# Sums by destination with two PSUM pairs for the slot results and the placement one step ahead

## The chip, the cores and the metric

The kernel runs on one core of one Trainium2 chip. The metric is the device time of one execution in microseconds (us). Three runs of the kernel before took 5358.63, 5363.5 and 5366.24 us, median 5363.5.

## The reference

Four graph layers run over one graph of 100,000 nodes with 16 features and 50,000 edges; each ends in `x = layernorm(x + layer(x))`. Edges are sorted by destination, and destinations are denser at small node numbers (`dst = 100000 * u**2`).

```python
# layer 0: attention over the edges of a destination (16x16 weights per edge)
e1, e2 = w_m * feat[src], w_a * feat[src]
ft = segment_sum(e1 * softmax_by_dst(e2), dst).sum(axis=1)
# layer 1: bilinear messages, added at the SOURCE node
messages = einsum('eu,ev,uvw->ew', x[row], x[col], W_tp);  out.at[row].add(messages)
# layer 2: two rounds of a graph convolution
agg = segment_sum(x[src], dst);  h = relu((x + agg) @ wa + ba) @ wb + bb      # twice
# layer 3: a 16x16 matrix per edge type (8 types), then a GRU cell
msg = einsum('emh,eh->em', edge_emb[edge_type], features[src])
m = segment_sum(msg, dst);  h_new = gru(m, features)
```

So `segment_sum(table[src], dst)` is computed three times: from the outputs of layer 1, of the first round of layer 2 and of the whole of layer 2. These are the three "sums by destination"; the third one also multiplies every gathered row by the matrix of its edge type.

## The kernel before

Five engines run their own instruction lists, written out by hand and tied by semaphores. Stages follow one another: the attention layer, node passes over 14 tiles of 7168 nodes, a sum by source, then three times a sum by destination followed by a node pass (`sum_by_destination(k)` and `node_steps`, k = 0, 1, 2).

Inside one sum by destination:

* **Gathers (GpSimd, L667).** The 50,176 padded edges stand in 392 tiles of 128. One indirect DMA for each tile fetches the 128 source rows into `dy`. They are issued in 49 groups of eight. Each group has its semaphore; SyncE waits for the group's landing (L583) and raises `tiles_ready`.
* **Slots.** The result lies in `acc` (SBUF) in 98 blocks of 1024 nodes. A slot is a pair of an edge tile and a block into which that tile writes; slots stand in order of tile and block, eight to a slot group, and there are 62 slot groups. Since a tile that crosses a block has two slots, the last slot groups need fewer new tiles than the first.
* **`pick` (ScalarE, L832)** waits until the last tile that its slot group needs is there, loads eight offsets into registers, and copies the eight picked row sets into `ysl[b]`, a PSUM buffer (two of them, in the pair `ps[3]`).
* **`place` (VectorE, L1526)** multiplies the picked rows with a mask, so that each row stands in the columns of its node within a group of eight (`placed[b]`, 128x1024).
* **`one_hot` (VectorE, L1519)** makes the matrix `oneh[b]` that maps an edge to its row of `acc`, from `io_p` in PSUM.
* **`slots` (TensorE, L1085)** multiplies `oneh[b]` by `placed[b]`, eight matmuls in two halves of four, into the PSUM pair `ps[2]`. `slot_ps` is raised after each half. Before each half it waits on `acc_done` until `collect` has read the same half of the slot group before.
* **`collect` (VectorE, L1543)** adds the eight results to `acc` at offsets held in registers, one after the other, each add waiting for the one before.

VectorE's step for slot group c is, in this order: `place(c)`, `one_hot(c+1)`, `collect(c)`. In the first two sums steps 2 to 59 are a hardware loop of two steps a turn, in the third all 62 are written out.

The third sum has for each tile group g also: `place_types(g)` on VectorE (a mask, L1504, then the rows spread over the eight types, L1509, called `zt`; it waits for `tiles_ready`), `turn` on TensorE (L1062, eight transposes into the pair `ps[0]`), `turned` on ScalarE (L807, `ps[0]` to SBUF), `messages` on TensorE (L1072) into `ps[1]` and on ScalarE (L813) back over `dy`. Only then can `pick` copy. Step n holds `place_types(n+3)` on VectorE between `place` and `one_hot`; on TensorE `turn(n+2)`, `messages(n+1)`, `slots(n)` in this order; on ScalarE `turned(n+2)`, `messages(n+1)`, `pick(n+1)`. Tile groups end with `place_types(48)` in step 45, `turn(48)` in step 46 and `messages(48)` in step 47, so steps 48 to 61 have slot work alone.

Of the kernel before, what the change touches and what calls it, by code (L numbers as in the profile page):

```python
# [30 lines left out]
ALU = mybir.AluOpType  # L31
# [3 lines left out]
P = 128  # L35
# [32 lines left out]
SG = 8  # L68
# [28 lines left out]
def build_program(nc, x, ef, wlog, repcon, src_t, dst_t, next_t, src_row, dst_row, prev_row, type_row, first_row,  # L97
# [3 lines left out]
    with ctx:  # L101
# [9 lines left out]
        def dram(name, shape, dt=FP32):  # L111
# [179 lines left out]
            sem(n) for n in ("tmask_done", "zt_done", "ztT_ps", "ztT_sb", "ym_ps", "msg_done"))  # L291
        ACC_ZEROS = 1

        node_in, late_in, stored = pair("node_in"), pair("late_in"), pair("stored")
# [653 lines left out]
        def _(pe):  # L948
# [102 lines left out]
            def sum_by_destination(k):  # L1051
# [24 lines left out]
                def slots(i, c):  # L1076
                    b = c % 2
                    pe.wait_ge(oneh_done, 2 * i + base + c + 1)
                    pe.wait_ge(placed_done, 2 * i + base + c + 1)
                    for h in range(2):  # L1080
                        if later(i, c, 1) or k:
                            pe.wait_ge(acc_done, 2 * SG * i + SG * (base + c - 1) + SG // 2 * (h + 1)
                                       + ACC_ZEROS * (k + later(i, c, 1)))
                        for j in range(SG // 2 * h, SG // 2 * (h + 1)):
                            last = pe.matmul(ps[2][:, j * P:(j + 1) * P], oneh[b][:, j * P:(j + 1) * P],  # L1085
                                             placed[b][:, j * P:(j + 1) * P], start=True, stop=True)
                        last.then_inc(slot_ps, 1)
# [91 lines left out]
        def _(dve):  # L1179
# [303 lines left out]
            def sum_by_destination(k):  # L1483
# [38 lines left out]

                def place(i, c):
                    b = c % 2
                    dve.wait_ge(y_copied, 2 * i + base + c + 1)
# [7 lines left out]
                def collect(i, c):  # L1533
# [4 lines left out]
                    for j in range(SG):  # L1538
# [3 lines left out]
                        o = acc[:, bass.ds(at[j], P)]  # L1542
                        dve.tensor_tensor(o, o, ps[2][:, j * P:(j + 1) * P], ALU.add).then_inc(acc_done, 1)  # L1543

                def step(i, c):
                    place(i, c)
                    if typed:
                        place_types(c + 3)
                    one_hot(i, c + 1)
                    collect(i, c)  # L1550

                if typed:
                    for g in range(3):
                        place_types(g)
                one_hot(0, 0)
                if typed:
                    for n in range(SLOT_GROUPS):
                        step(0, n)
                else:
                    steps(dve, step, 0, 2, SLOT_GROUPS - 2, SLOT_GROUPS)  # L1560
# [213 lines left out]
```

## Time and profile before

| | before |
|---|---|
| median of three runs | 5363.5 us |
| profiled execution | 5358.86 us |
| its span, first to last instruction | 5357.0 us |
| VectorE busy | 3796.2 us (71%) |
| TensorE matmul busy | 3260.3 us (61%) |
| GpSimd busy | 3045.7 us (57%) |
| ScalarE busy | 1645.2 us (31%) |
| mean granted TensorE clock | 0.77 of full |

About 2 us of the profiled execution lie outside its span. Busy shares are averages over stages with different limits. The three sums by destination, which the change touches, take some 530, 530 and 632 us, and in each of them another engine may be the one that the others wait for; the views of those stretches tell which.

### The profile page before, as it was taken

Reading aid. Unit: us, or ns where it says so; the run is one execution under the profiler, and the core shown is the slowest. Engines: PE = TensorE matmul, PEld = TensorE weight load, DVE = VectorE, ACT = ScalarE, POOL = GpSimd, SP = SyncE. Lnnn points to the kernel's source line nnn. Section 1 sums busy time; section 2 is a strip of 40 time slices with the busy share of each in tenths; the row PEclk is TensorE's granted clock in tenths of the full one; section 3 lists DMA queues with packets and bytes.
Section 4 is the critical chain, followed back from the end, with each engine's and each line's share of the span. In section 5 each row is a group of like instructions: output and inputs, shape, how many; then the busy total and the mean of one; then the engine's idle time right before and its main releaser. Section 6 shows DMA issues by size and latency. Waiting matters only on the chain.

```text
span 5357.0 us, 56936 instructions
## 1 busy us (share of the span) xinstructions
PE 3260.3 (61%) x12357; PEld 2396.4 (45%) x12357; DVE 3796.2 (71%) x6342; ACT 1645.2 (31%) x4066; POOL 3045.7 (57%) x2659
## 2 busy tenths in 40 slices
PE   5888888888805344436878444453444544766686
PEld 2444444444405334435767334443344324666432
DVE  5999999999966555536999755644556674555588
ACT  2555555555532111102333101111111341222143
POOL 2666666666612888885555677715777007776000
PEclk9999999999995665558999655676556565666598
DMA  3111111111142444431211000041000320000122
GB/s 93 36 44 42 38 44 41 41 41 44 27 111 53 57 58 62 59 40 36 55 41 51 14 7 7 7 116 35 7 7 7 103 86 10 7 7 7 35 82 75
DMA packets 400935, 231.46 MB, mean 43 GB/s; under 512 B 127626, under 2 KB 365646, under 8 KB 400802
## 3 DMA queue, kind: packets, MB, share of 16 engines
q1 hardware_dynamic: 281522, 210.43, 13.8%
q0 software_dynamic: 119296, 19.68, 6.8%
q8 instruction: 48, 0.79, 0.1%
q14 instruction: 69, 0.57, 0.0%
HBM read 152.10 MB, written 58.54 MB: 39 GB/s over the span
## 4 chain that ended last, share of the span: by engine, by line
POOL 34%; DVE 26%; issue 19%; PE 9%; DMA 6%; ACT 2%; SPq 2%; DVEq 1%; POOLq 0%; ACTq 0%
POOL extra L667 21%; POOL sums L652 9%; DVE arena L1599 4%; POOL xg L630 3%; DMA sums<-cmb,sidx 3%; DVE arena L1323 2%; DVE arena L1347 2%; PE ps L1127 2%; PE ps L994 2%; DMA edge_in<-far_row 2%; POOL ft_t L619 1%; PE ps L1085 1%; DVE arena L1543 1%; DVE ps L1317 1%; DVE arena L1331 1%
## 5 line engine op out<-in xcount | busy, mean ns | idle before, releaser
L1085 PE MATMUL ps<-arena 128*128 128x128 f32 x2976 | 687.0, 424 | 764.2 <-DVE arena L1526 692.7
L667 POOL DMA_INDIRECT extra<-x_t,srci x784 | 780.1, 995 | 527.0 <-issue 527.0
L1085 PEld LDWEIGHTS ps<-arena 128*128 128x128 f32 x2976 | 638.3, 326 | 804.9 <-issue 804.9
L652 POOL DMA_INDIRECT sums<-cmb,sidx x392 | 613.6, 1565 | 336.4 <-ACT cmb L781 204.3
L994 PE MATMUL ps<-edge_in,wl 17*128 17x512 f32 x784 | 704.4, 1076 | 87.3 <-DMA edge_in<-far_row 85.1
L1543 DVE TENSOR_TENSOR arena<-arena,ps 128x128 f32 x1488 | 427.8, 287 | 368.3 <-PE ps L1085 193.1
L630 POOL DMA_INDIRECT xg<-in_x,xidx x392 | 437.5, 1116 | 353.1 <-DVE xp L1305 233.4
L619 POOL DMA_INDIRECT ft_t<-fts,fidx x392 | 506.7, 1293 | 139.2 <-issue 117.6
L1032 PE MATMUL ps<-arena 128*128 128x128 f32 x992 | 226.8, 421 | 521.1 <-DVE arena L1410 521.1
L667 POOL DMA_INDIRECT extra<-h_t,srci x392 | 383.4, 978 | 251.5 <-issue 251.5
L832 ACT ACTIVATE ps<-extra 128x16 f32 x1488 | 171.3, 168 | 1066.1 <-SPq L583 868.6
L994 PEld LDWEIGHTS ps<-edge_in,wl 17*128 17x128 f32 x784 | 243.5, 325 | 479.3 <-issue 352.5
L1032 PEld LDWEIGHTS ps<-arena 128*128 128x128 f32 x992 | 210.7, 323 | 529.4 <-DVE arena L1410 529.4
L1127 PE MATMUL ps<-wb,arena 128*128 128x256 f32 x1568 | 389.9, 406 | 91.8 <-ACT arena L860 76.4
L976 PE MATMUL ps<-cst,arena 128*128 128x16 f32 x1568 | 351.2, 375 | 111.4 <-ACT fts L709 101.0
L976 PEld LDWEIGHTS ps<-cst,arena 128*128 128x128 f32 x1568 | 341.9, 331 | 132.3 <-issue 121.5
L1127 PEld LDWEIGHTS ps<-wb,arena 128*128 128x128 f32 x1568 | 312.2, 204 | 144.4 <-ACT arena L860 95.7
L1526 DVE TENSOR_TENSOR arena<-edge_in,ps 128x1024 f32<-128x1024 f32 (+1 forms) x186 | 226.7, 1219 | 169.1 <-ACT ps L832 159.5
L394 POOL TENSOR_TENSOR extra<-arena 128x512 f32<-128x512 f32 x196 | 203.3, 1058 | 245.1 <-DVE arena L1599 230.2
L1599 DVE TENSOR_REDUCE arena<-extra 128x32 f32<-128x512 f32 x294 | 282.3, 1016 | 0.0
L1323 DVE TENSOR_TENSOR_SCAN arena<-ps,arena,edge_in 128x512 f32<-128x512 f32 x196 | 240.8, 1271 | 13.4
L1519 DVE TENSOR_TENSOR arena<-ps,relp 128x1024 f32<-128x1024 f32 x186 | 226.3, 1216 | 0.1
(200 smaller groups left out, 5978.9 us busy)
## 6 DMA issues: line engine op xcount, KB each, us to landing
edge_in<-far_row SPq DMA_DIRECT2D x98, 256.0 KB
ain<-in_src_row SPq DMA_DIRECT2D x56, 448.0 KB, 3.9
sums<-zero SPq DMA_DIRECT2D x132, 144.0 KB
ain<-arena SPq DMA_DIRECT2D x42, 448.0 KB, 5.2
arena<-rel_t SPq DMA_DIRECT2D x63, 256.0 KB, 4.0
x_t<-yout SPq DMA_DIRECT2D x28, 448.0 KB, 3.3
extra<-x_t,srci POOLq DMA_INDIRECT x784, 2.4
xin<-x_t SPq DMA_DIRECT2D x28, 448.0 KB, 4.7
```

The costliest lines, as they stand in the source:

```text
L619: pool.indirect_dma_start(ft_t, bass.IndirectOffsetOnAxis(ap=fidx[b][:, k:k + 1], axis=0), fts[b][:, k * F:(k + 1) * F], None).then_inc(ft ...
L630: pool.indirect_dma_start(xg[:, k, :], None, x, bass.IndirectOffsetOnAxis(ap=xidx[:, k:k + 1], axis=0)).then_inc(x_gathered, 16)
L652: pool.indirect_dma_start(sums[k], bass.IndirectOffsetOnAxis(ap=sidx[n % 2][:, j:j + 1], axis=0), cmb[n % 2][:, j, :], None, compute_op=AL ...
L667: pool.indirect_dma_start(dy[:, t, :], None, table, bass.IndirectOffsetOnAxis(ap=srci[:, t:t + 1], axis=0)).then_inc(d_gathered[n % QUEUE] ...
L976: last = pe.matmul(ps[3][:, 512 + k * F:512 + (k + 1) * F], rat[b][:, h, k * P:(k + 1) * P], selo, start=h == 0, stop=h == CH - 1)
L994: last = pe.matmul(ps[k][:, h * ET:(h + 1) * ET], wl[:, (k * CH + h) * P:(k * CH + h + 1) * P], eft[b][:, :], start=True, stop=True)
L1032: last = pe.matmul(ps[b][:, j * P:(j + 1) * P], turned_oneh[b][:, j * P:(j + 1) * P], xblk[b][:, j * P:(j + 1) * P], start=True, stop=True)
L1085: last = pe.matmul(ps[2][:, j * P:(j + 1) * P], oneh[b][:, j * P:(j + 1) * P], placed[b][:, j * P:(j + 1) * P], start=True, stop=True)
L1127: last = pe.matmul(bank_of(k)[:, 256 * s:256 * (s + 1)], sT[par_], wbk[j // 4][:, (j % 4) * 256:(j % 4 + 1) * 256], start=True, stop=True)
L1323: last = dve.tensor_tensor_scan(mx[b][:, h, 1:ET + 1], ps[0][:, h * ET:(h + 1) * ET], far[b][:, :], mx[b][:, h, 0:1], ALU.max, ALU.add)
L1543: dve.tensor_tensor(o, o, ps[2][:, j * P:(j + 1) * P], ALU.add).then_inc(acc_done, 1)
L1599: dve.tensor_reduce(slots(zz)[:, s0:s0 + 2, :], ([prod[n_par(c, g)]] + pool_prod)[k].rearrange("p (s u w) -> p s w u", s=2, u=F), AX, ALU. ...
```

## The change

`slot_sums(k, n)` names the PSUM pair into which slot group n of sum k goes. In the first two sums it is `ps[2]` for even and `ps[0]` for odd groups. In the third it is `ps[2]` up to group 50, since `turn` uses `ps[0]`, and from group 51 on the two alternate; the first group in `ps[0]` waits until `ztT_sb` shows that `turned` has read all. `back` is how many groups back the `collect` lies that must have read the pair: 2 where the pairs alternate, else 1.

VectorE's step for slot group c becomes `place(c+1)`, `one_hot(c+2)`, `collect(c)`. `place(0)` and `one_hot(1)` move ahead of the first step. `one_hot(c+2)` writes the buffer that `slots(c)` reads, and waits for both its halves. The picked rows stay in `ysl` in PSUM, as before. No operation is added or removed, only waits change.

```diff
--- before.py
+++ after.py
@@ -290,6 +290,13 @@
         tmask_done, zt_done, ztT_ps, ztT_sb, ym_ps, msg_done = (
             sem(n) for n in ("tmask_done", "zt_done", "ztT_ps", "ztT_sb", "ym_ps", "msg_done"))
         ACC_ZEROS = 1
+        TYPES_DONE = TILE_GROUPS + TILE_GROUPS % 2
+
+        def slot_sums(k, n):
+
+            if k < DST_PASSES - 1:
+                return ps[0] if n % 2 else ps[2]
+            return ps[0] if n > TYPES_DONE and n % 2 else ps[2]
 
         node_in, late_in, stored = pair("node_in"), pair("late_in"), pair("stored")
         v_done, s_own, s_xm, s_sq, s_ve, s_sd, y_done = (
@@ -1075,14 +1082,18 @@
 
                 def slots(i, c):
                     b = c % 2
+                    n = c
+                    back = 2 if not typed or n > TYPES_DONE + 1 else 1
+                    if typed and n == TYPES_DONE + 1:
+                        pe.wait_ge(ztT_sb, TILE_GROUPS)
                     pe.wait_ge(oneh_done, 2 * i + base + c + 1)
                     pe.wait_ge(placed_done, 2 * i + base + c + 1)
                     for h in range(2):
-                        if later(i, c, 1) or k:
-                            pe.wait_ge(acc_done, 2 * SG * i + SG * (base + c - 1) + SG // 2 * (h + 1)
-                                       + ACC_ZEROS * (k + later(i, c, 1)))
+                        if later(i, c, back) or k:
+                            pe.wait_ge(acc_done, 2 * SG * i + SG * (base + c - back) + SG // 2 * (h + 1)
+                                       + ACC_ZEROS * (k + later(i, c, back)))
                         for j in range(SG // 2 * h, SG // 2 * (h + 1)):
-                            last = pe.matmul(ps[2][:, j * P:(j + 1) * P], oneh[b][:, j * P:(j + 1) * P],
+                            last = pe.matmul(slot_sums(k, n)[:, j * P:(j + 1) * P], oneh[b][:, j * P:(j + 1) * P],
                                              placed[b][:, j * P:(j + 1) * P], start=True, stop=True)
                         last.then_inc(slot_ps, 1)
 
@@ -1521,6 +1532,8 @@
                                       ALU.is_equal).then_inc(oneh_done, 1)
 
                 def place(i, c):
+                    if not inside(i, c, SLOT_GROUPS):
+                        return
                     b = c % 2
                     dve.wait_ge(y_copied, 2 * i + base + c + 1)
                     dve.tensor_tensor(
@@ -1540,19 +1553,21 @@
                             dve.wait_ge(slot_ps, 4 * i + 2 * (base + c) + j // (SG // 2) + 1)
                         dve.wait_ge(acc_done, 2 * SG * i + SG * (base + c) + j + ACC_ZEROS * (k + 1))
                         o = acc[:, bass.ds(at[j], P)]
-                        dve.tensor_tensor(o, o, ps[2][:, j * P:(j + 1) * P], ALU.add).then_inc(acc_done, 1)
+                        dve.tensor_tensor(o, o, slot_sums(k, c)[:, j * P:(j + 1) * P], ALU.add).then_inc(acc_done, 1)
 
                 def step(i, c):
-                    place(i, c)
+                    place(i, c + 1)
                     if typed:
                         place_types(c + 3)
-                    one_hot(i, c + 1)
+                    one_hot(i, c + 2)
                     collect(i, c)
 
                 if typed:
                     for g in range(3):
                         place_types(g)
                 one_hot(0, 0)
+                place(0, 0)
+                one_hot(0, 1)
                 if typed:
                     for n in range(SLOT_GROUPS):
                         step(0, n)
```

VectorE at the start of the first sum, before (L1490 clears `acc`, L1492 makes the mask, L1519 is `one_hot`, L1526 `place`, TENSOR_LOAD the offsets for `collect`, ISA a wait, L1543 an add of `collect`):

```order
L1490 MEMSET arena 128x12672
L1492 TENSOR_TENSOR edge_in<-cst,relj 128x3968
L1519 TENSOR_TENSOR arena<-ps1,relp 128x1024
L1526 TENSOR_TENSOR arena<-edge_in,ps3 128x1024
L1519 TENSOR_TENSOR arena<-ps1,relp 128x1024
L1534 TENSOR_LOAD offs
L1543 ISA
L1543 TENSOR_TENSOR arena<-arena,ps2 128x128
```

The same place in the changed kernel (its lines are L1501, L1503, L1530 `one_hot`, L1539 `place`, L1556 `collect`):

```order
L1501 MEMSET arena 128x12672
L1503 TENSOR_TENSOR edge_in<-cst,relj 128x3968
L1530 TENSOR_TENSOR arena<-ps1,relp 128x1024
L1539 TENSOR_TENSOR arena<-edge_in,ps3 128x1024
L1530 TENSOR_TENSOR arena<-ps1,relp 128x1024
L1539 TENSOR_TENSOR arena<-edge_in,ps3 128x1024
L1530 TENSOR_TENSOR arena<-ps1,relp 128x1024
L1547 TENSOR_LOAD offs
L1556 ISA
L1556 TENSOR_TENSOR arena<-arena,ps2 128x128
```

One more `place` and one more `one_hot` stand ahead of the first `collect`, and from there on each `collect` comes behind the placement of the next slot group.

TensorE at the end of the third sum, in the changed kernel (L1079 is `messages(48)`, L1096 `slots`):

```order
L1079 MATMUL ps1<-prm,arena 128x16 x8
L1096 MATMUL ps2<-arena 128x128 x32
L1096 MATMUL ps0<-arena 128x128 x8
L1096 MATMUL ps2<-arena 128x128 x8
L1096 MATMUL ps0<-arena 128x128 x8
L1096 MATMUL ps2<-arena 128x128 x8
L1096 MATMUL ps0<-arena 128x128 x8
L1096 MATMUL ps2<-arena 128x128 x8
```

In the kernel before the last of these rows is a single one:

```order
L1062 MATMUL ps0<-cst,arena 128x128 x8
L1072 MATMUL ps1<-prm,extra 128x16 x8
L1085 MATMUL ps2<-arena 128x128 x8
L1072 MATMUL ps1<-prm,arena 128x16 x8
L1085 MATMUL ps2<-arena 128x128 x120
```

Of the 15 slot groups from 47 on, the four up to 50 still go to `ps2` and the last eleven alternate between the pairs, beginning and ending with `ps0`.

## Rows read from the trace of the kernel before

**Rows 1.** The page, chain that ended last, shares of the span by line.
```profile
POOL extra L667 21%; POOL sums L652 9%; DVE arena L1599 4%; POOL xg L630 3%; DMA sums<-cmb,sidx 3%; DVE arena L1323 2%; DVE arena L1347 2%; PE ps L1127 2%; PE ps L994 2%; DMA edge_in<-far_row 2%; POOL ft_t L619 1%; PE ps L1085 1%; DVE arena L1543 1%; DVE ps L1317 1%; DVE arena L1331 1%
```

**Rows 2.** Windows over the three sums: span; busy PE, PEld, DVE, ACT, POOL; clock.
```profile
3013.00:3543.00 530.00, 228.46 (x992) 211.72 (x992) 301.93 (x622) 56.90 (x496) 383.41 (x392) 0.59 0.08 6
3648.00:4178.00 530.00, 228.14 (x992) 211.36 (x992) 302.06 (x622) 56.91 (x496) 383.38 (x392) 0.58 0.08 6
4425.00:5057.00 632.00, 401.39 (x2168) 381.17 (x2168) 360.66 (x720) 121.17 (x594) 396.64 (x392) 0.61 0.08 6
```

**Rows 3.** Line L667, first and third sum: ns min/median/max, first and last start.
```profile
L667 POOL DMA_INDIRECT extra<-x_t,srci x784: 940/944/14406, 3013.7 to 4939.9; - x196
```

**Rows 4.** Timeline, end of the first sum: start us, us, engine, line, operation.
```profile
3515.34 0.94 POOL L667 DMA_INDIRECT extra<-x_t,srci  x1 [0.30 <-issue]
...
3518.60 0.92 ACT L832 ACTIVATE ps<-extra 128x16 f32 x8 [9.70 <-SPq L583]
...
3521.47 1.22 DVE L1526 TENSOR_TENSOR arena<-edge_in,ps 128x1024 f32<-128x1024 f32 x1
...
3540.66 1.55 DVE L1543 TENSOR_TENSOR arena<-arena,ps 128x128 f32 x4 [0.20 <-PE ps L1085]
```

**Rows 5.** Timeline, end of the second sum.
```profile
4153.55 0.92 ACT L832 ACTIVATE ps<-extra 128x16 f32 x8 [9.76 <-SPq L583]
...
4175.99 1.55 DVE L1543 TENSOR_TENSOR arena<-arena,ps 128x128 f32 x4 [0.20 <-PE ps L1085]
```

**Rows 6.** Timeline, an ordinary step of the third sum.
```profile
4612.85 1.26 DVE L1509 TENSOR_TENSOR arena<-tmask,extra 128x1024 f32<-128x1024 f32 x1 [3.06 <-SPq L583]
...
4614.04 1.21 DVE L1519 TENSOR_TENSOR arena<-ps,relp 128x1024 f32<-128x1024 f32 x1
...
4614.17 1.09 PE L1062 MATMUL ps<-cst,arena 128*128 128x128 f32 x8 [0.66 <-DVE arena L1509]
...
4615.18 1.53 DVE L1543 TENSOR_TENSOR arena<-arena,ps 128x128 f32 x4
...
4619.13 0.92 ACT L832 ACTIVATE ps<-extra 128x16 f32 x8 [1.86 <-issue]
...
4622.76 1.23 DVE L1509 TENSOR_TENSOR arena<-tmask,extra 128x1024 f32<-128x1024 f32 x1 [3.04 <-SPq L583]
4622.85 1.96 POOL L667 DMA_INDIRECT extra<-x_t,srci  x1 [0.30 <-issue]
```

**Rows 7.** Timeline, a step of the third sum in which TensorE ran slower.
```profile
4633.78 1.22 DVE L1509 TENSOR_TENSOR arena<-tmask,extra 128x1024 f32<-128x1024 f32 x1 [4.20 <-SPq L583]
...
4642.47 0.92 ACT L832 ACTIVATE ps<-extra 128x16 f32 x8 [1.89 <-issue]
```

**Rows 8.** Windows over TensorE's turn and messages in those two steps.
```profile
4614.17:4616.96 2.79, 2.79 (x24) 2.69 (x24) 2.20 (x6) 1.02 (x1) 2.18 (x3) 1.00 0.09 6
...
4635.06:4640.26 5.20, 5.20 (x24) 5.09 (x24) 4.21 (x10) 1.03 (x1) 3.98 (x5) 0.50 0.07 5
```

**Rows 9.** Line L1509, tile groups 3 to 48: ns min/median/max, first and last start.
```profile
L1509 DVE TENSOR_TENSOR arena<-tmask,extra x46: 1224/1246/1296, 4480.6 to 4943.1; 128x1024 f32<-128x1024 f32 x46
```

**Rows 10.** Timeline, end of the third sum, with one whole step.
```profile
4951.55 0.92 ACT L832 ACTIVATE ps<-extra 128x16 f32 x8 [1.88 <-issue]
...
4989.29 1.21 DVE L1526 TENSOR_TENSOR arena<-edge_in,ps 128x1024 f32<-128x1024 bf16 x1
4990.42 1.22 DVE L1519 TENSOR_TENSOR arena<-ps,relp 128x1024 f32<-128x1024 f32 x1
...
4990.60 3.76 PE L1085 MATMUL ps<-arena 128*128 128x128 f32 x16 [2.94 <-DVE arena L1526]
...
4992.78 1.54 DVE L1543 TENSOR_TENSOR arena<-arena,ps 128x128 f32 x4 [1.15 <-PE ps L1085]
...
4995.99 1.21 DVE L1526 TENSOR_TENSOR arena<-edge_in,ps 128x1024 f32<-128x1024 bf16 x1
...
5056.80 0.38 SPq L503 DMA_DIRECT2D edge_in<-x_t  x1
```

## The prediction

> **What bounds the kernel now.** I read the chain that ended last first. Its largest entry is the gather of the sums by destination, L667, with 21% of the span [rows 1], three sums of 530, 530 and 632 us [rows 2]. VectorE is busy for 302 of the 530 us, TensorE for 228 [rows 2], so neither fills the first two sums. GpSimd does: one gather takes 0.94 us [rows 3] and 0.30 us pass before the next [rows 4], so 391 gathers at 1.25 us and the first, which takes 14.4 us [rows 3], make 502 us. From 3013.7 [rows 3] that leads to the last one at 3515.3 [rows 4]. What VectorE does faster before that moment is worth nothing. What counts is how long each sum goes on after its last gather: to 3542.2 in the first (3540.66 + 1.55), to 4177.5 in the second [rows 5]. The third starts its last `zt` (tile group 48) at 4943.1 [rows 9] and ends at 5056.8 [rows 10]: 113.7 us, long after the last gather. That tail is where slot work alone sets the time.
>
> **The slot step and what the change saves on it.** In the tail a step lasts from one `place` to the next, 4989.29 to 4995.99, 6.70 us [rows 10]. In it `one_hot` starts 1.13 us after `place` and ends at 4991.64. TensorE starts at 4990.60, once `place` is done, and `collect` begins only at 4992.78, 1.15 us idle for the first four products; from there to the next `place` 3.21 us pass [rows 10]. Where the products are ready, `collect` starts 1.14 us after `one_hot` (4614.04 to 4615.18) [rows 6]. So a step that never waits takes 1.13 + 1.14 + 3.21 = 5.48 us, 1.22 less. With the pairs alternating and `place` one step ahead, TensorE has a whole step of 5.48 us for its 3.76 us [rows 10]; it isn't the limit.
>
> *Third sum, tail.* I count from the start of `collect(50)` to the end.
> - Before: three starts of `collect` lie between steps 50 and 53, and the full step of [rows 10] is step 52 (place(52) at 4989.29, ten places before the end). Going back two steps from 4992.78 gives 4979.4, so 77.4 us to the end.
> - Until group 50 there is one pair. `slots(n)` can then start its halves behind those of `collect(n-1)`: 1.55 + 0.15 us after that start, 3.76 us long, and only then `one_hot(n+2)`, whose buffer it read, 1.14 us before `collect(n)`: 1.70 + 3.76 + 0.1 + 1.14 = 6.7 us. So steps 47 to 51 gain nothing, the wait only moves from `collect` to `one_hot`.
> - From group 52 the step is 5.48. Steps 52 to 59 are eight: 43.8 us. Step 60 has no `one_hot`: 3.21 + 1.2 = 4.4. For the last, the offsets are loaded with nothing beside it (I take 0.5 us): 3.7, and its own adds 3.3. With the 6.7 of step 51 this is 61.9 us, 15.5 less.
> - Against it, `place(47)` now stands a step earlier than the rows it needs. `pick(47)` ends at 4951.55 + 0.92 = 4952.47 [rows 10]; `collect(46)` then starts at 4952.6 + 2.27 = 4954.9. Before, counting back six steps of 6.7 from 4992.78, it starts at 4952.6 at most, its `place` 3.5 us ahead, so VectorE now waits some 4 us for the pick. Some 2.5 us late, which nothing behind it makes up.
> - Net: 13 us less.
>
> *First and second sum, tail.* The last group of tiles frees `pick(59)`, which ends at 3518.60 + 0.92 = 3519.5, and `place(59)` starts at 3521.5 since VectorE is still in the step before [rows 4]: 22.7 us from that pick to the end. After the change VectorE waits there instead: place(59) at 3519.65, `collect(58)` 2.27 later, `collect(59)` 5.5 on, `collect(60)` 4.6 (a loop's end of 0.2 in it), `collect(61)` 3.7 and 3.3 for its adds: 19.5 us, 3.2 less, although there is one more `collect` behind the last pick. Likewise the second: 4153.55 + 0.92 to 4177.5 is 23.1 [rows 5], so 3.6 less. Together 6.8. The bounds: at least 0, if the added collect eats it all, and 9 if steps overlap better than I count.
>
> *Third sum, up to `zt(48)`.* The moved `place(n+1)` stands ahead of the `zt` that waits for the gathers, so `pick` must now be early enough. In the ordinary step the pick that follows a `zt` at 4612.85 ends at 4620.05, 7.2 us on [rows 6]; `place` (0.12 + 1.13) and the mask (0.3) bring the next `zt` to 8.8 us at the earliest. The gathers allow one `zt` in (4943.1 - 4480.6)/45 = 10.28 us [rows 9]. With TensorE slower, the pick ends at 4643.39, 9.6 us after the `zt` [rows 7], and the next `zt` would be 11.2 us on. The difference is TensorE's clock: the same 24 instructions took 2.79 us at 2.4 GHz (1.00) and 5.20 us at 1.2 GHz (0.50) [rows 8]. If a share p of steps is slow, 8.8 + 2.4 p exceeds 10.28 beyond p = 0.6. Before, slow steps are the minority, and the mean clock of this sum is 0.61 [rows 2]. Now `slots(n)` follows `messages(n+1)` at once instead of 2.7 us later, and TensorE then idles in one piece of 2 to 4 us up to the next `turn`. I take that slow and ordinary steps mix about evenly: nothing gained, 1 us lost. Bounds: 45 x (11.2 - 10.28) = 41 us lost, and 13 us gained if all stalls of the gathers (below) vanish.
>
> The Trainium skill (TensorE: Matmul & The Clock Gate, section "HAM oscillation — how this bites in real kernels") says that pauses between batches of matmuls throttle the engine again and again. By this rule, which speaks against gathering the idle time, the `turn` would always start slow. The sum up to `zt(48)` would then be the 41 us bound.
>
> **Sum.** -13 - 6.8 + 1 = -18.8 us. The profiled execution took 5358.9, 2 us more than its span and 4.6 us under the median of the runs. Against the median of 5363.5 the forecast is 5345 us.
>
> **The rivals.**
> *A, the late pick becomes the bound of the third sum.* Every step before `zt(48)` runs at the lower clock and lasts 11.2 us: +41 - 19.8 = +21, 5385 us. For it: the freed time lies in one idle piece ahead of `turn`, and in [rows 7, 8] such a step exists. Against it: `turn`, `messages` and `slots` now form one unbroken block of 7 to 9 us, the most continuous work TensorE has had in this sum. It decides from p = 0.6 on. 12 in 100.
>
> *B, more gathers stall.* A gather issued 0.09 us after a `zt` started took 1.96 instead of 0.94 us [rows 6], and in the third sum the gathers were busy 396.6 against 383.4 us in the others [rows 2]: 13.2 us of such stalls. `place`, `one_hot` and `collect` each have an operand in PSUM, and the first two sums, which have only these, have no stall. At present `zt` starts where a gather has just been issued, mostly a hair late for the next. If late picks move it by some tenths of a us, each of the 45 may meet a gather in its middle and hold it for 0.6 us, half of its own 1.25: 27 us instead of 13, so 14 us later. Then 5345 + 14 = 5359, within 0.2% of before. 17 in 100.
> The Trainium skill (SBUF — State Buffer, section "SBUF: two separate sides") says that a VectorE operation with two SBUF inputs and a GpSimd operation that reads SBUF exclude each other for the whole instruction. The trace agrees for the `zt`; its 14.4 us for the first gather beside the clearing of `acc` fits too [rows 3].
>
> *C, fewer stalls.* The same shift moves `zt` past the gather that it now hits. Then up to 13 us more come off, 5334 us. 13 in 100.
>
> *D, it doesn't do what it says,* since the first two sums gain nothing and the third's last steps go on waiting, for `one_hot` or for TensorE at 3.76 us a group: 5345 + 13 = 5358. 8 in 100: eight steps of 5.48 would have to be near 6.7.
>
> **How the numbers follow.** Forecast 50, A 12, B 17, C 13, D 8. The range reaches from C to just above B: 5334 to 5366 us. About what a measurement of this kernel can tell from no change is 0.2%, 10.7 us. Faster than 5352.8: forecast and C, and a bit of B and D, less the upper part of the forecast: 0.67. Slower than 5374: A, 0.11. The rest, 0.22, is the same.
>
> **What will show it.** In the third sum's tail, places from step 53 on about 5.5 us apart and adds of `collect` with no idle time ahead of them; steps 47 to 51 still 6.7 apart. `place(47)` behind its pick with some 4 us idle. The last `zt` within a few us of 4943 relative to the start of that sum at 4425. The end of the first sum about 19.5 us after the pick of its last tiles. I'm wrong if the `zt`s of the third sum lie more than 10.5 us apart on average, with `place` waiting for `pick` ahead of each (A), if L667 is busy for over 405 us there (B) or under 390 (C).

## The result, and the profile after

The changed kernel took 5348.37 us (median of 20 runs, 5338.56 to 5356.92), the kernel before 5361.15 us beside it (20 runs, 5354.73 to 5372.6). The ratio is 0.9974, 95% interval 0.9968 to 0.9981: 14 us (10 to 17) faster. Forecast were 5345 us and 18.8 us less. The profiled execution took 5352.29 us, its span is 5350.5 us.

Lines have moved: gathers are L674, SyncE's wait L590, `turned` L814, `pick` L839, `turn` L1069, `messages` L1079, `slots` L1096, `zt` L1520, `one_hot` L1530, `place` L1539, `collect` L1556.

The chain that ended last is of less use here. Its shares add up to a fifth of the span only, so its 8% for the gathers can't be held against the 21% in [rows 1]; their busy time did not fall.

```profile
POOL 8%; DVE 7%; issue 4%; PE 2%; ACT 1%; DMA 0%; DVEq 0%; ACTq 0%; POOLq 0%; SPq 0%
```

So I read windows over the three sums, as in [rows 2] (stretch; its length; busy PE, PEld, DVE, ACT, POOL; granted clock; DMA share; GB/s), and the starts of gathers and of `zt` (ns min/median/max, first and last start), as in [rows 3, 9]:

```profile
3010.00:3540.00 530.00, 217.46 (x992) 201.41 (x992) 296.04 (x622) 56.90 (x496) 383.35 (x392) 0.60 0.08 8
3640.00:4170.00 530.00, 220.41 (x992) 204.04 (x992) 295.90 (x622) 56.88 (x496) 383.34 (x392) 0.60 0.08 8
4413.00:5053.00 640.00, 442.99 (x2168) 425.56 (x2168) 363.89 (x720) 121.16 (x594) 412.84 (x392) 0.60 0.07 7
```

```profile
L674 POOL DMA_INDIRECT extra<-x_t,srci x784: 940/944/14414, 3010.2 to 4945.1; - x196
L1520 DVE TENSOR_TENSOR arena<-tmask,extra x49: 1224/1225/1291, 4438.8 to 4948.3; 128x1024 f32<-128x1024 f32 x49
...
  SPq L590: 48.1, 23
```

The last line is the time that VectorE sat idle ahead of these `zt`s for SyncE's word that the gathers had landed, and how often. The kernel before had:

```profile
  SPq L583: 188.3, 49
```

GpSimd is as busy as before in the first two sums, and 16.2 us busier in the third (412.84 against 396.64). From the third sum's first gather (4414.0, 4425.0 before) to its last `zt` it is now 534.3 us, 518.1 before: the same 16.2 us. Of the 49 `zt`s 23 still wait for gathers; before, all 49 did.

The end of the first sum, for [rows 4], and of the second, for [rows 5]:

```profile
3515.07 0.92 ACT L839 ACTIVATE ps<-extra 128x16 f32 x8 [9.65 <-SPq L590]
3516.16 1.22 DVE L1539 TENSOR_TENSOR arena<-edge_in,ps 128x1024 f32<-128x1024 f32 x1 [4.11 <-ACT ps L839]
...
3518.43 3.21 DVE L1556 TENSOR_TENSOR arena<-arena,ps 128x128 f32 x8
...
3523.85 3.21 DVE L1556 TENSOR_TENSOR arena<-arena,ps 128x128 f32 x8
...
3533.77 1.54 DVE L1556 TENSOR_TENSOR arena<-arena,ps 128x128 f32 x4 [0.20 <-DVE arena L1556]
...
4144.94 0.92 ACT L839 ACTIVATE ps<-extra 128x16 f32 x8 [9.79 <-SPq L590]
...
4163.57 1.54 DVE L1556 TENSOR_TENSOR arena<-arena,ps 128x128 f32 x4 [0.20 <-DVE arena L1556]
```

VectorE, 4.1 us idle, now waits for the pick instead of arriving late; from the pick's end (3515.99) to the last add (3535.31) it is 19.3 us, and in the second sum 19.25. They were 22.7 and 23.1.

The tail of the third sum, for [rows 10]: `place(47)` behind its pick, a step before group 51, then an ordinary step and the end.

```profile
4957.00 0.92 ACT L839 ACTIVATE ps<-extra 128x16 f32 x8 [1.87 <-issue]
4957.95 1.22 DVE L1539 TENSOR_TENSOR arena<-edge_in,ps 128x1024 f32<-128x1024 bf16 x1 [4.05 <-ACT ps L839]
...
4963.42 1.21 DVE L1539 TENSOR_TENSOR arena<-edge_in,ps 128x1024 f32<-128x1024 bf16 x1
...
4965.34 1.23 DVE L1530 TENSOR_TENSOR arena<-ps,relp 128x1024 f32<-128x1024 f32 x1 [0.71 <-PE ps L1096]
...
4969.68 1.21 DVE L1539 TENSOR_TENSOR arena<-edge_in,ps 128x1024 f32<-128x1024 bf16 x1
...
5023.85 1.21 DVE L1539 TENSOR_TENSOR arena<-edge_in,ps 128x1024 f32<-128x1024 bf16 x1
5024.98 1.22 DVE L1530 TENSOR_TENSOR arena<-ps,relp 128x1024 f32<-128x1024 f32 x1
...
5026.11 1.53 DVE L1556 TENSOR_TENSOR arena<-arena,ps 128x128 f32 x4
...
5029.31 1.21 DVE L1539 TENSOR_TENSOR arena<-edge_in,ps 128x1024 f32<-128x1024 bf16 x1
...
5048.85 0.38 SPq L510 DMA_DIRECT2D edge_in<-x_t  x1
```

The step is 5.46 us (5023.85 to 5029.31), and `collect` follows `one_hot` without idle time. Ahead of group 51 it is 6.26 here and up to 6.9 later: the idle time stands ahead of `one_hot`. From the last `zt` to the end it is 100.5 us, 113.7 before.

So the tails gave back 3.4 + 3.8 + 13.2 = 20.4 us, and in this pair of executions the stretch before the last `zt` took 16.2 of them. The measured gain is 14 us. The spans differ by 6.5 us, 5357.0 against 5350.5; the 2.3 us beyond that 4.2 lie outside the sums. What the 16.2 us are is the question of the experiments.

### The profile page after: what moved, and what is told of

Read it like the earlier page. It is cut to its first block and busy times, and to the rows that moved or that the text cites. A ratio compares the mean times of both kernels' runs of the same rounds, so it can differ in the third digit from the quotient of the medians.

```text
span 5350.5 us, 56879 instructions
## 1 busy us (share of the span) xinstructions
PE 3291.9 (62%) x12357; PEld 2431.8 (45%) x12357; DVE 3786.6 (71%) x6342; ACT 1645.3 (31%) x4066; POOL 3062.1 (57%) x2659
## 5 line engine op out<-in xcount | busy, mean ns | idle before, releaser
L674 POOL DMA_INDIRECT extra<-x_t,srci x784 | 796.2, 1016 | 524.7 <-issue 524.7
L1096 PE MATMUL ps<-arena 128*128 128x128 f32 x2976 | 661.0, 412 | 667.0 <-DVE arena L1539 603.4
L1096 PEld LDWEIGHTS ps<-arena 128*128 128x128 f32 x2976 | 614.6, 314 | 703.1 <-issue 699.8
L1539 DVE TENSOR_TENSOR arena<-edge_in,ps 128x1024 f32<-128x1024 f32 (+1 forms) x186 | 226.9, 1220 | 496.5 <-ACT ps L839 489.9
L1556 DVE TENSOR_TENSOR arena<-arena,ps 128x128 f32 x1488 | 425.8, 286 | 179.6 <-DVE arena L1556 18.8
L1039 PE MATMUL ps<-arena 128*128 128x128 f32 x992 | 228.1, 423 | 511.7 <-DVE arena L1421 511.7
L674 POOL DMA_INDIRECT extra<-h_t,srci x392 | 383.3, 978 | 246.5 <-issue 246.5
L839 ACT ACTIVATE ps<-extra 128x16 f32 x1488 | 171.2, 168 | 1055.7 <-SPq L590 874.5
L1039 PEld LDWEIGHTS ps<-arena 128*128 128x128 f32 x992 | 211.4, 324 | 520.2 <-DVE arena L1421 520.2
L1530 DVE TENSOR_TENSOR arena<-ps,relp 128x1024 f32<-128x1024 f32 x186 | 226.3, 1217 | 4.8 <-PE ps L1096 4.7
```

Source lines behind the costliest of these rows:

```text
L674: pool.indirect_dma_start(dy[:, t, :], None, table, bass.IndirectOffsetOnAxis(ap=srci[:, t:t + 1], axis=0)).then_inc(d_gathered[n % QUEUE] ...
L1039: last = pe.matmul(ps[b][:, j * P:(j + 1) * P], turned_oneh[b][:, j * P:(j + 1) * P], xblk[b][:, j * P:(j + 1) * P], start=True, stop=True)
L1096: last = pe.matmul(slot_sums(k, n)[:, j * P:(j + 1) * P], oneh[b][:, j * P:(j + 1) * P], placed[b][:, j * P:(j + 1) * P], start=True, stop ...
L1556: dve.tensor_tensor(o, o, slot_sums(k, c)[:, j * P:(j + 1) * P], ALU.add).then_inc(acc_done, 1)
```

## The experiments

A gather is called stalled when it takes longer than the usual 0.944 us. The expectations name four theories:

* **Theory S:** in the third sum a `zt` holds back a gather issued while it runs, since `zt` reads two operands in SBUF. In the expectations of e1 to e4 it also says that the new order brings more of this.
* **Theory B:** that second half alone, under its own name from f_after on.
* **Theory V:** how often it happens is a draw of each execution, not the work of the new order.
* **Theory C:** with placement ahead the pick's own chain (`zt`, `turn`, `messages`, `pick`, `place`) limits the typed steps of the third sum, those that hold a `place_types`.

The table is worked out from the traces, in us. "Gathers": busy time of the 392 gathers of the third sum. "Last zt": from the first gather of that sum to the start of the last `zt`. "Ends": from the pick of the last tiles to the last add, first and second sum. "Tail": from the last `zt` to the last add.

| kernel | gathers | last zt | ends | tail | ratio to before, interval |
|---|---|---|---|---|---|
| before | 396.6 | 518.1 | 22.7, 23.1 | 113.7 | 1 |
| changed | 412.8 | 534.3 | 19.3, 19.3 | 100.5 | 0.9974 (0.9968, 0.9981) |
| f_after (the same again) | 408.8 | 530.9 | 19.4, 19.3 | 100.9 | 0.9969 (0.9958, 0.9981) |
| e1_late_switch | 404.9 | 526.4 | 19.3, 19.3 | 100.9 | 0.9968 (0.9956, 0.9980) |
| e2_first_two_only | 410.5 | 531.9 | 19.3, 19.3 | 113.2 | 0.9993 (0.9984, 1.0002) |
| e3_ahead_one_pair | 412.1 | 533.6 | 20.6, 20.5 | 110.1 | 0.9993 (0.9983, 1.0002) |
| e4_pairs_old_order | 414.8 | 536.3 | 22.7, 23.2 | 112.5 | 0.9995 (0.9986, 1.0004) |
| f6_before_mask_psum | 383.3 | 504.8 | 22.7, 22.9 | 113.6 | 0.9954 (0.9941, 0.9968) |
| f5_after_mask_psum | 383.6 | 508.8 | 19.3, 19.3 | 101.0 | 0.9929 (0.9915, 0.9943) |
| f8_late_psum_49 | 383.3 | 504.8 | 19.4, 19.3 | 97.8 | 0.9916 (0.9902, 0.9929) |

### e1_late_switch and e2_first_two_only: the old order in the third sum

e1 keeps the old order there up to step 46 and places ahead from 47; e2 keeps it to the end, and one PSUM pair with it. In both the `place(0)` and `one_hot(1)` ahead of the first step are left out in the third sum (not in the cuts shown).

```diff
 # e1_late_switch
-                        step(0, n)
+                        if n < 47:
+                            place(0, n)
+                            place_types(n + 3)
+                            one_hot(0, n + 1)
+                            collect(0, n)
+                        else:
+                            if n == 47:
+                                place(0, n)
+                                one_hot(0, n + 1)
+                            step(0, n)
 # e2_first_two_only
-        TYPES_DONE = TILE_GROUPS + TILE_GROUPS % 2
+        TYPES_DONE = SLOT_GROUPS
...
-                        step(0, n)
+                        place(0, n)
+                        place_types(n + 3)
+                        one_hot(0, n + 1)
+                        collect(0, n)
```

> The third sum keeps the old order (place(n), zt, one_hot(n+1)) up to step 46 and places ahead only from step 47 on; all else as changed. Theory S (stalled gathers: zt, started by the pick instead of by the landing, holds up more gathers): L667's gathers in the third sum are busy 397 +-4 us instead of 412.8, the last zt lies 518 +-4 us after the first gather instead of 534, the tail from it stays at 101 +-2, so some 13 to 19 us come off the changed kernel: ratio to before 0.9960 +-0.0010. Theory C (the late pick itself bounds the step): the same place of the last zt, since the pick is off the path again; this run doesn't part S and C. Theory V (chance: the two profiles fell on different draws): gathers 405 to 413 us here too, ratio 0.9974.

> Two pairs and placement ahead in the first two sums alone, the third sum as before. All theories that take the tail of the first two sums for the gain: 19.3 us instead of 22.7 and 23.1 from the pick of the last tiles to the end, 7 us together, ratio 0.9987 +-0.0007. The third sum 632 +-5 us, its gathers 397 +-4 us busy. If the first two sums' gain were eaten somewhere (rival), ratio 1.0000.

Measured: e1 has the changed kernel's tail (100.9) and its ratio; expected under S were gathers of 397 us and 0.9960. e2 keeps the old tail (113.2) and 3.8 us of gain (interval -1 to 9), where the two ends are worth 7. But their gathers were busy for 404.9 and 410.5 us with the order of the kernel before, which had shown 396.6. So it isn't the new order that brings such stalls: the old order has them too, and theory S as it then stood, with about 397 for both kernels, failed.

### e3_ahead_one_pair and e4_pairs_old_order: each half of the change alone

```diff
 # e3_ahead_one_pair
-        TYPES_DONE = TILE_GROUPS + TILE_GROUPS % 2
+        TYPES_DONE = SLOT_GROUPS
...
-                return ps[0] if n % 2 else ps[2]
-            return ps[0] if n > TYPES_DONE and n % 2 else ps[2]
+                return ps[2]
+            return ps[2]
...
-                    back = 2 if not typed or n > TYPES_DONE + 1 else 1
+                    back = 1
 # e4_pairs_old_order
-                    place(i, c + 1)
+                    place(i, c)
...
-                    one_hot(i, c + 2)
+                    one_hot(i, c + 1)
...
-                place(0, 0)
-                one_hot(0, 1)
```

> Placement one step ahead in all three sums, but every slot result in the one pair ps2. My theory (both parts are needed): the wait moves from collect to one_hot, steps of the third sum's tail stay 6.6 to 6.7 us apart, the end of that sum lies 113 us or more behind its last zt, and the gathers are busy 405 to 415 us as in the changed kernel. The first two sums gain 0 to -1 us each at their ends. Ratio 1.0020 to 1.0040, slower than before. Rival (placement ahead alone brings the gain, the pairs nothing): tail steps of 5.5 us, ratio 0.9975.

> Two pairs as in the changed kernel, but VectorE in the old order (place(c), one_hot(c+1), collect(c)). My theory: slots(c) still can't start before place(c), 1.3 us after it, so each tail step stays 6.7 us, the gathers are busy 397 +-4 us, ratio 1.0000 +-0.0007. Rival (the pairs alone bring the gain): tail steps of 5.5 us, ratio 0.9965.

A step in the tail of e3 (placement ahead, one pair), and one of e4 (two pairs, the old order):

```profile
5020.58 1.21 DVE L1539 TENSOR_TENSOR arena<-edge_in,ps 128x1024 f32<-128x1024 bf16 x1
...
5022.85 1.23 DVE L1530 TENSOR_TENSOR arena<-ps,relp 128x1024 f32<-128x1024 f32 x1 [1.06 <-PE ps L1096]
5023.99 1.53 DVE L1556 TENSOR_TENSOR arena<-arena,ps 128x128 f32 x4
...
5025.67 4.08 PE L1096 MATMUL ps<-arena 128*128 128x128 f32 x16 [2.86 <-DVE arena L1556]
```

```profile
5018.41 1.21 DVE L1539 TENSOR_TENSOR arena<-edge_in,ps 128x1024 f32<-128x1024 bf16 x1
5019.54 1.22 DVE L1530 TENSOR_TENSOR arena<-ps,relp 128x1024 f32<-128x1024 f32 x1
...
5021.91 1.54 DVE L1556 TENSOR_TENSOR arena<-arena,ps 128x128 f32 x4 [1.15 <-PE ps L1096]
```

With one pair TensorE waits for `collect` and `one_hot` then waits 1.06 us for TensorE; with two pairs in the old order `collect` waits 1.15 us, as in [rows 10]. Either half alone leaves a step of 6.6 to 6.7 us and neither ratio can be told from 1. Only both together take the 1.2 us out. e3's tail also shows the prediction's account of steps 47 to 51, placement ahead with one pair.

Two expectations missed. e3 was to be slower than before (1.0020 to 1.0040), with ends at most 1 us shorter and a tail of 113 us or more; its ends are 2.1 and 2.6 us shorter and its tail is 110.1. So placement ahead alone does shorten the last steps by some 8 us in all, while its time gained 4 (-1 to 9). e4's gathers were to be busy for 397 us and took 414.8, the most of all, in the old order.

### f_after, f5_after_mask_psum, f6_before_mask_psum, f8_late_psum_49: `zt`'s mask in PSUM

The mask that `zt` reads beside the gathered rows moves from SBUF into free columns of a PSUM pair; nothing else changes, and `zt` still takes 1.22 us. f5 is the changed kernel with it, f6 the kernel before, f8 is e1 with it and with the third sum's pairs alternating from group 49 on.

```diff
 # f5, f6, f8
-        tmask = [sb(f"tmask{b}", [P, SG, TYPES]) for b in range(2)]
+        tmask = [ps[1][:, 640 + 64 * b:704 + 64 * b].rearrange("p (s k) -> p s k", s=SG) for b in range(2)]
 # f8 also, beside the edit of e1
-        TYPES_DONE = TILE_GROUPS + TILE_GROUPS % 2
+        TYPES_DONE = TILE_GROUPS - TILE_GROUPS % 2
```

> The changed kernel itself, once more, beside the kernel before. Theory V (the number of gathers that stall in the third sum is a draw of each execution; placement one step ahead adds at most a few us to it): ratio 0.9974 +/- 0.0015 as in the first comparison; gathers of the third sum busy 405 to 415 us. Theory B (placement ahead itself makes 16 us of stalls): gathers 411 to 415, never below. A value below 408 speaks against B.

> The changed kernel with the per-type mask of the third sum (tmask, which zt reads) in PSUM in place of SBUF. Theory S (gathers stall beside zt because zt reads two operands of SBUF): gathers of the third sum busy 384 to 388 us as in the first two sums, last zt at 505 to 510 us from the sum's first gather if the gathers alone set the pace, ratio near 0.992. Theory C (with placement ahead the late picks also set the pace): gathers 384 to 390, but last zt at 515 to 530, ratio 0.993 to 0.997. On a chip in the regime of the first run of this kernel (6449 us): gathers unchanged at 407 to 413, last zt near 975, ratio 1.000.

> The kernel before with the per-type mask in PSUM. Theory S: gathers of the third sum busy 384 to 388, last zt at 505 to 508, ratio 0.996. If the operand's place does not matter: gathers 397 to 415, ratio 1.000.

> First two sums as in the changed kernel; third sum in the old order up to step 46, placement one step ahead from 47, its two PSUM pairs alternating from group 49; mask in PSUM. Theory S and C alike: last zt as in the kernel before with the mask in PSUM, the third sum's tail 97 us, first two sums' tails 19.3 us: 6.8 + 16 less, and another 10 to 20 us if the mask's place frees the gathers: ratio 0.992 +/- 0.002. If the mask's place is worth nothing: 0.9955.

Windows over the third sum of f_after, f5, f6 and f8 (POOL is the last busy time):

```profile
4416.00:5056.00 640.00, 444.22 (x2173) 426.37 (x2174) 364.68 (x720) 121.26 (x594) 408.76 (x392) 0.59 0.07 8
```
```profile
4413.00:5053.00 640.00, 456.55 (x2231) 429.96 (x2232) 371.01 (x752) 127.44 (x601) 383.58 (x392) 0.61 0.09 13
```
```profile
4420.00:5060.00 640.00, 437.10 (x2199) 411.11 (x2200) 363.58 (x733) 122.99 (x596) 383.30 (x392) 0.59 0.08 12
```
```profile
4419.00:5059.00 640.00, 439.67 (x2246) 407.23 (x2247) 370.77 (x766) 127.79 (x601) 383.34 (x392) 0.62 0.09 13
```

With the mask in PSUM the gathers of the third sum are as fast as those of the first (383.3 to 383.6): theory S, the cause, holds. f6, the kernel before with this one edit, gains 0.46%, 25 us, more than the change itself. And the spread of its runs falls: 5340.64 to 5344.31 us over five, where the kernel before ranged over 5359.45 to 5373.46 in eleven beside it; f8 ranges over 4.5 us, but f5 over 13.0, with one run at 5336.96. So the stalls are likely the larger part of the scatter of the kernel before, but five runs don't show it. That the number of stalls is drawn anew in each execution, theory V, rests on the old order's four totals (396.6 to 414.8).

f_after doesn't decide between V and B: its gathers took 408.8 us, under the 411 below which B was never to fall, and above the 408 under which a value was to speak against B.

What `zt`s wait for in f5, and in f6:

```profile
L1520 DVE TENSOR_TENSOR arena<-ps,extra x49: 1224/1224/1226, 4439.1 to 4923.2; 128x1024 f32<-128x1024 f32 x49
...
  SPq L590: 29.9, 5
```
```profile
L1509 DVE TENSOR_TENSOR arena<-ps,extra x49: 1224/1225/1226, 4446.4 to 4926.5; 128x1024 f32<-128x1024 f32 x49
...
  SPq L583: 176.0, 49
```

Once the gathers are free, only 5 of 49 `zt`s still wait for them in f5; the others start right behind `place`, so behind the pick. The steps last 10.07 us on average instead of 10.00 and the last `zt` is 4.0 us late (508.8, 504.8). Theory C's mechanism exists, but is worth less here than its 10 to 25 us. f5 against f6 is the change without stalls: 5326.35 for 5342.47 us, 16 less by the medians (14 by the means, for f5's one slow run); ends and tail give 20 (7.0 and 12.6) and the late picks take 4. f8 avoids that by the old order up to step 46, and gains 3 us in the tail by using the second pair two groups earlier. With 5323.62 us against 5365.41 (-0.84%) it is the fastest here, though its lead of 3 us over f5 (5326.35) lies within the intervals.

### e5 to e8: the same edits on another chip

e5_after_mask_psum, e6_before_mask_psum and e8_late_psum_49 are the kernels of f5, f6 and f8; e7_late_mask_psum is e8 without the alternation from group 49. They ran ahead of the f runs, which are the same questions asked again.

> The changed kernel, with the type mask (tmask, the second operand of zt) in PSUM instead of SBUF, so that zt has one SBUF input alone. Theory S (a zt holds up a gather issued into it): the stalls go, L674's gathers of the third sum are busy 384 to 388 us instead of 412.8 (the small mask operation may still cost a little). If the pick's chain doesn't bind, the last zt lies 505 to 508 us after the first gather, and the ratio to before is 0.9925 +-0.0010. Theory C (the late pick bounds the step as well): gathers 384 to 388 too, but the last zt only at 515 to 530, with place starting 0.03 us after its pick in each step, ratio 0.994 to 0.997. If zt isn't what holds the gathers up: 405 to 415 us busy, ratio 0.9974.

> The kernel before, with the type mask in PSUM. Theory S: gathers of the third sum busy 384 to 388 us, last zt 505 to 508 us after the first gather instead of 518 to 536, tail 113 us as before: 20 us off on average, ratio 0.9962 +-0.0010. If zt isn't what stalls the gathers: 397 to 415 us, ratio 1.0000.

> Old order in the third sum up to step 46, placement ahead from step 47 on, and the type mask in PSUM. Theories S and C alike: last zt 505 to 508 us after the first gather, tail 101 us, ratio 0.9925 +-0.0010. Against e5 it parts them: under S alone both are equal, under C this one is 8 to 20 us faster.

> As e7, with the third sum's pairs alternating from slot group 49 on instead of 51 (turned(48) has read ps0 by then). If a tail step without the second pair costs 6.6 us and one with it 5.46: two more steps gain, 2.3 us off the tail, 98.5 us, ratio 0.9920 +-0.0010. If the first step in ps0 must wait for turned(48): no gain.

These four ran on a chip on which the kernel before took 6449.28 us, so their times can be compared only with that one and among themselves. The ratios were 1.0000 (0.9990, 1.0009), 1.0002 (0.9992, 1.0011), 0.9785 (0.9771, 0.9799) and 0.9785 (0.9771, 0.9799). The mask's place couldn't be judged here: the gathers took 407 to 414 us in all three sums of all four, the first two included, which have no `zt`, for 384 to 388 expected. Windows over the third sum of e5:

```profile
5100.00:5400.00 300.00, 28.39 (x112) 26.49 (x112) 14.39 (x26) 6.93 (x31) 228.18 (x232) 0.50 0.08 6
5400.00:5700.00 300.00, 86.15 (x400) 82.72 (x400) 61.59 (x123) 23.10 (x108) 142.62 (x133) 0.52 0.04 4
5700.00:6030.00 330.00, 262.40 (x1334) 253.20 (x1334) 197.60 (x400) 74.30 (x331) 0.00 (x0) 0.62 0.00 1
```

TensorE, VectorE and ScalarE nearly stand still while GpSimd gathers (28, 14 and 7 us of the first 300), and catch up when it is done, 534 us after its first gather. In the timeline of e7 the matmuls of `messages` come one at a time:

```profile
5318.13 0.19 PE L1079 MATMUL ps<-prm,extra 128*128 128x16 f32 x1 [3.31 <-issue]
...
5320.92 0.18 PE L1079 MATMUL ps<-prm,extra 128*128 128x16 f32 x1 [2.60 <-issue]
...
5323.72 0.18 PE L1079 MATMUL ps<-prm,extra 128*128 128x16 f32 x1 [2.62 <-issue]
```

2.6 us pass before each, without a wait that the profile shows, in step with two gathers. What starves the engines there was not settled; that instructions arrive late behind the gathers is a guess from these rows.

The last `zt` came 975 us after the first gather in e5, 842 in e6, e7 and e8. This difference of 133 us does not arise while the engines are starved: the first `zt` after the last gather starts 565 us after the first gather in e5 and 567 in e6 and e7, and 41 and 40 are still to come. It is these that differ, when no gather is left to wait for:

```profile
5617.00:6027.00 410.00, 326.71 (x1640) 315.09 (x1640) 243.21 (x495) 91.41 (x410) 0.00 (x0) 0.61 0.00 1
```
```profile
5628.00:5902.00 274.00, 240.81 (x1591) 238.50 (x1591) 232.25 (x479) 88.47 (x399) 0.00 (x0) 0.76 0.01 1
```

The first row is of e5, 41 steps of 9.99 us; the second of e7, 40 steps of 6.88 us in the old order, and e6's are as long. In e5 each `place` waits for its pick, and the next `zt` stands behind it:

```profile
5658.28 1.22 DVE L1539 TENSOR_TENSOR arena<-edge_in,ps 128x1024 f32<-128x1024 bf16 x1 [4.04 <-ACT ps L839]
...
5659.68 1.22 DVE L1520 TENSOR_TENSOR arena<-ps,extra 128x1024 f32<-128x1024 f32 x1
```

So this is theory C at its full price: with placement ahead the pick's chain makes a typed step 10 us, 3.1 us more than the old order needs, and on the chips of the other runs the gathers hid it, since they allow no step under 10.0 us anyway. The first two sums, which have no typed steps, show the other side. The steps behind the last gather of the first sum, 48 in e5 and 49 in e6, take 5.6 us in e5 and 6.9 in e6, and that sum lasts 831 against 897 us. This is the prediction's saving of 1.2 us a step, at work in most steps of a sum and not in its last few. By these traces the first two sums give 131 us and the third takes 122, so the change gains and loses about as much: e5 and e6 both have a ratio of 1.000. The expected values did not reckon with such a stage.

## Why the prediction was right

The sign held, and so did the two terms that make the gain; one term was mis-sized. The time (5348 for 5345) looks better than the gain (14 us for 18.8), by luck: the three runs from which the forecast started have a median 2.4 us above that of all twenty. By the prediction's own signs, the profiled execution is not the forecast case but rival B: gathers busy for over 405 us. Its `zt`s also lie 10.6 us apart, past the 10.5 of rival A, though 23 of them waited for gathers and not for the pick.

- **Third sum, tail, -13.** Measured -13.2. The step of 5.48 is 5.46, steps up to 51 stayed slow with the wait moved to `one_hot`, and `place(47)` waits 4.05 us for its pick, forecast some 4. The last two steps took 4.33 and 4.18 us for 4.4 and 3.7.
- **First and second sum, -3.2 and -3.6.** Measured -3.4 and -3.8. `place(59)` starts 0.17 us behind the pick's end, `collect(58)` 2.27 later, `collect(59)` 5.42, as worked out.
- **Up to `zt(48)`, +1, bounds -13 and +41.** This is the mis-sized term. In the profiled pair it was +16.2, all of it stalled gathers: what they took beyond 0.944 us each, the first one left out, was 13.1 us before and 29.3 after. That is rival B's mark and its size (27 us), though not its step: B had each of 45 gathers held for 0.6 us, and here 33 were held by more than 0.1 us, most of them for about 1 us. In all seven profiled executions with the mask in SBUF the last `zt` lies 505 to 506 us plus the stalls behind the first gather, so nothing else moved it. The old order in e1, e2 and e4 showed stalls of 21.4, 27.0 and 31.3 us, the new order in f_after and e3 25.3 and 28.6. The means are 23.2 for the old order (four executions) and 27.7 for the new one (three): +4.5 us, which with a spread of 18 us within the old order these profiles don't show; and e2, e3 and e4 were profiled in the slowest of their eleven runs, which makes their totals high ones. The times say a little more. Ends and tail give back 20 us in each pair of traces, and the twenty runs of each kernel gained 14 (10 to 17), so 3 to 10 us went elsewhere, if the other stages took the same time; f_after's runs (17, 10 to 23) leave that open. So the term is nearer 5 us than 1. The 13 us of [rows 2, 6] on which I built both B and C were a low draw of one execution.
- **The late pick.** I put the chain pick, `place`, `zt` at 8.8 + 2.4 p us with p about one half, 10.0 us against the gathers' 10.28, and called it nothing. Free of stalls it measures 10.07 (f5), and 9.99 with no gathers to wait for (e5), so the sum was right and the margin nil: it costs 4 us as soon as the gathers are free of stalls. In the changed kernel eight transposes of a `turn` took under 1.2 us in 17 of the last 45 steps and over 1.9 in 23, before in 38 and 7, and the granted clock of the steps fell from 0.65 to 0.58:

```profile
4480.00:4943.00 463.00, 317.30 (x1800) 301.98 (x1800) 263.86 (x540) 100.20 (x450) 351.39 (x360) 0.65 0.09 7
```
```profile
4477.00:4948.00 471.00, 363.75 (x1773) 351.04 (x1771) 262.38 (x530) 98.89 (x448) 361.46 (x354) 0.58 0.08 7
```

The first row is of before, the second of after; TensorE is busy for 46 us longer with the same work. That is rival A's mechanism, in part and without its price.
- **Rival C's time.** It is added up wrongly: -13 - 6.8 - 13 from 5363.5 is 5331 us, not 5334, and the lower end of the range rests on it.

With the mean for the stalls, the sum is -20.4 + 4.5 = -15.9 us, for a measured -14 (-17 to -10) and in f_after -17 (-23 to -10). By the single pair of profiles it would be -4.

Two rules of the Trainium skill had been weighed. By "HAM oscillation — how this bites in real kernels" (TensorE: Matmul & The Clock Gate), where pauses between batches of matmuls throttle the engine again and again, every `turn` would have started slow. The clock did fall, but in f5 one `turn` took 1.10 us and the next 1.97, so some start fast.

```profile
4686.17 1.10 PE L1069 MATMUL ps<-cst,arena 128*128 128x128 f32 x8 [2.48 <-DVE arena L1520]
...
4695.75 1.97 PE L1069 MATMUL ps<-cst,arena 128*128 128x128 f32 x8 [2.20 <-DVE arena L1520]
```

By the Trainium skill's "SBUF: two separate sides" (SBUF — State Buffer) a VectorE operation with two SBUF inputs and a GpSimd operation that reads SBUF exclude each other for the whole instruction. With one input in PSUM 397 to 415 us became 383, so f5, f6 and f8 agree on the cause; on the size the last section differs from it.

The prediction also took the 14.4 us of the first gather as a case of this rule. That isn't shown. In the changed kernel's trace this gather is issued 1.24 us into the clearing of `acc` (10.62 us), which reads nothing from SBUF, and lasts until 0.88 us after the operation behind it (4.23 us), which has two SBUF inputs. The rule as quoted speaks of the second operation only; what held the gather beside the first stays open.

## What to carry to other kernels

When one engine issues something at a fixed pace and another starts just as it has been issued, a few hundredths of a us decide whether the two collide, and one profiled execution says little of how often: here the old order alone gave 13 to 31 us. Before a stall count enters a sum, look at its spread over executions, or better take its cause away and see what it was worth: here one operand moved to PSUM was worth more than the change. A double buffer and an earlier producer may each be worth nothing while the other is missing, and an order that gains where no one waits can be kept out of the steps in which its input comes late. Where one engine's pace only just hides a chain of others, as the gathers' 10.0 us a step hides the pick's chain of 10.0 here, the chain costs little until that engine is done; on the chip of e5 to e8 it was, and the change lost in one sum about all that it won in two.

## What the runs showed of the hardware

A gather issued x us after the start of a `zt` with both operands in SBUF takes longer by about 1.1 - x us, for x from about 0.05 to 1.1. Over seven executions 132 gathers issued 0.05 to 0.15 us after it took 1.89 to 2.0 us, three at 0.4 took 1.59 to 1.68, six at 0.8 took 1.21 to 1.28, and from 1.1 on they took 0.94 to 0.99. In the changed kernel's trace:

```profile
4574.60 1.22 DVE L1520 TENSOR_TENSOR arena<-tmask,extra 128x1024 f32<-128x1024 f32 x1
...
4575.05 1.59 POOL L674 DMA_INDIRECT extra<-x_t,srci  x1 [0.30 <-issue]
...
4584.43 1.26 DVE L1520 TENSOR_TENSOR arena<-tmask,extra 128x1024 f32<-128x1024 f32 x1
...
4584.44 0.94 POOL L674 DMA_INDIRECT extra<-x_t,srci  x1 [0.30 <-issue]
```

The gather 0.45 us behind its `zt` is held for 0.65 us; the one issued with it, 0.01 us behind, is not, and the `zt` takes 1.26 instead of 1.22; over all of them no `zt` took more than 1.30. So the `zt` holds the gather, and the gather hardly the `zt`. The Trainium skill states more in "SBUF: two separate sides" (SBUF — State Buffer): there whichever starts first blocks the other for its whole instruction. The other surprise was the chip of e5 to e8, where the same kernel took 20% longer, and the order of the third sum's typed steps, e5 against e7, moved the time by 2.2%, since most of them ran with no gather to wait for; f5 against f8 moved it by 0.1%.
